# A graph network of four blocks on one core: pooling laid into the attribute pass, and overflow tiles of layer 1 made by comparison

## The chip, the core and the metric

The kernel runs as one program on one core of a Trainium2 chip. The metric is the device time of one execution in microseconds, the median of several runs. The engines are TensorE (PE in the profile), VectorE (DVE), ScalarE (ACT), GpSimd (POOL) and SyncE (SP). SP, and here ScalarE too, issue DMAs whose descriptors the hardware makes; GpSimd issues the indirect DMAs.

## What is computed

There are 12500 nodes with 64 features and 212500 edges, sorted by destination. Every block normalises the node rows, computes, and adds its result to x:

```python
h = relu(layernorm(x)); x = x + L0(h)  # max over edges in both directions of relu(h[.] * (1 + coef*w) @ pool_w.T + b),
                                       # then relu(concat(h, max) @ final_w.T + final_b)
h = relu(layernorm(x)); x = x + L1(h)  # 4 layers: relu(norm(dinv * A^T (dinv * h @ W) + ...)), statistics over all nodes
h = relu(layernorm(x)); x = x + L2(h)  # sums over edges of relu parts of h[dst], vector v and edge weight, then W4
h = relu(layernorm(x)); x = x + L3(h)  # sum, max and mean of 32 edge attributes per source node, then two matrices
```

## The kernel before, in words

Nodes are laid out as NJ = 98 blocks of P = 128 rows, edges as TILES = 1664 columns of 128, worked in NCH = 208 chunks. `adj` in HBM holds the number of edges from source row to destination column as bytes, with NV = 7 further blocks of 128 "virtual" rows. A byte holds up to 255, so for each full 256 equal edges an overflow entry goes to a virtual row; that row stands for one source node (`srow`) and one column (`vcol`, -1 where there is none).

In order of time:

1. Edge pass 1 (GpSimd gathers, L854) and edge pass 2 (GpSimd scatters records, L908), until 4490.
2. GpSimd then works down one queue without a branch: 84 gathers of run ends, `adj_out` for the first 15 of NB = 52 batches (L934; a batch is 32 indirect DMAs of 128 one-byte writes each), a wait for edge pass 3, 98 gathers of run ends into AG, `adj_out` to batch 48, `virtual_rows` (seven gathers of the layer's table at `srow`, after a wait for the table), and the last four batches. When half of a batch is issued it waits for the one before to have landed and counts it in `cells_in`.
3. Beside it the other engines do edge pass 3, then the attribute pass: for each of 208 chunks SP loads records and, for each pair, masks; TensorE turns them (`attr_fwd`), ScalarE makes penalties from the masks (`attr_pen`), VectorE runs two scans of 512 columns (`attr_scans`), TensorE turns back (`attr_back`), ScalarE copies, SP stores. `RUNS_E` cuts the pass after 40 chunks. Between the two parts stands `project`: for 14 groups of seven blocks, `make_b` corrects the run maxima in T and AG and writes Z, TensorE turns Z, ScalarE copies, TensorE multiplies by `finalw`, `post_b` adds to X. Then `norm(NG2 + 2)` on VectorE.
4. Layer 1 in parts (`by_parts` on TensorE, L1322). `CUTS` divides the 98 source blocks into NCK = 9 parts of 30, 16, 14, 12, 8, 6, 5, 5 and 2 blocks (numbered 0 to 8 here). For each part and each of NG2 = 7 groups of 1792 columns (a unit), SP loads one raw tile of 128 x 1792 bytes for each block (L770), ScalarE (three of five, L1808) or VectorE (two of five, L2556/L2558) casts it to bf16 in a ring of NR = 5, and TensorE multiplies it with three bf16 terms, 12 matmuls. SP holds the loads of a part back until `cells_in` reaches a count `chk`, which for this graph is 17, 26, 33, 40, 44, 47, 50, 52 for parts 0 to 7 and NB + 1 = 53 for part 8. `add_part` on VectorE adds a unit's result to FM; for the units of part 8 `scaled` adds, multiplies with the broadcast 1/sqrt(degree) (DINVB, loaded by SP in `group_end`, which waits for `scaled` of the unit two before) and takes statistics. The seven virtual blocks are in part 8: 9 tiles a unit there, 63 in all. Layer 1 has 7 x 105 = 735 tiles.
5. Layers 2 to 4 (`dense`, L1342), then blocks L2 and L3 (L1532). Before the last phase VectorE writes `srj`, the column numbers shifted for each block, with 98 small tensor_scalars (L2796); there the virtual destination tiles are already made by a comparison of `iota_f` with `srj` (L2886).

Before part 8 VectorE's cast is a scalar_tensor_tensor that adds a column of zeros held in PSUM; in part 8 it is a tensor_copy:

```python
if r * NR + i >= LAST_FROM:
    dve.tensor_copy(RING[i], RAW[i]).then_inc(sem("conv_d"), 1)
else:
    dve.scalar_tensor_tensor(RING[i], RAW[i], 1.0, NOTHING.broadcast_to([P, 2 * QW]), ALU.mult, ALU.add)...
```

## Time and profile before

| | us |
|---|---|
| median of three runs | 9879.17 (9872.16 to 9879.8) |
| profiled execution | 9849.77, its span 9847.9 |
| busy in the span: PE, DVE | 7048.5, 7017.6 |
| busy in the span: POOL, ACT | 5374.9, 4868.2 |
| mean granted clock of TensorE | 0.77 |

All durations below are from that one profiled execution, in microseconds from the start of its span. A busy engine doesn't set the time by being busy: one asks in each stretch which engine or transfer the others wait for. "Idle before" is how long an engine sat idle before an instruction, with what released it.

### The profile page before, as it was taken

What the parts mean: (1) busy time and instruction counts of PE and PEld (TensorE: products, weight loads), DVE (VectorE), ACT (ScalarE), POOL (GpSimd) and SP (SyncE); (2) the same over time, 40 slices, a digit from 0 to 9 for tenths busy, and PEclk for the clock granted to TensorE, in tenths of its full rate; (3) what the DMA queues carried; (4) which work ended last, traced back from release to release, by engine and by line L of the source; (5) the groups of instructions that cost most, each with busy time, mean ns of one, the idle gap of its engine ahead of it and who ended that gap; (6) DMA issues with size and microseconds to landing.
All of it is one profiled execution on the core that took longest, in us unless ns stands there. A gap on an engine that the chain in (4) does not pass through costs nothing.

```text
span 9847.9 us, 151767 instructions
## 1 busy us (share of the span) xinstructions
PE 7048.5 (72%) x44134; PEld 5763.7 (59%) x44134; DVE 7017.6 (71%) x18590; ACT 4868.2 (49%) x7967; POOL 5374.9 (55%) x5426
## 2 busy tenths in 40 slices
PE   4444444424888878872656567996899999997998
PEld 3333333313666667661445455664699898896887
DVE  7888888833666666662558777775688787787777
ACT  1111111112555555551442336885688787785787
POOL 5777777777777777777777777776000000000220
PEclk5555555555777776775776788998999999998999
DMA  5556544444333333339995896775788888886999
GB/s 192 195 194 196 175 143 143 144 134 66 93 92 93 92 93 93 94 92 93 266 229 123 188 216 175 204 204 123 221 281 281 248 280 252 275 281 177 210 218 198
DMA packets 2775520, 1739.57 MB, mean 177 GB/s; under 512 B 1805046, under 2 KB 2613980, under 8 KB 2774660
## 3 DMA queue, kind: packets, MB, share of 16 engines
q1 hardware_dynamic: 2435460, 1298.36, 52.3%
q10 hardware_dynamic: 165920, 277.72, 8.1%
q0 software_dynamic: 173408, 154.46, 6.8%
q8 instruction: 370, 6.06, 0.3%
q14 instruction: 362, 2.97, 0.1%
HBM read 1065.70 MB, written 506.69 MB: 160 GB/s over the span
## 4 chain that ended last, share of the span: by engine, by line
POOL 44%; PE 19%; issue 18%; DMA 9%; DVE 5%; ACT 3%; SPq 1%; POOLq 0%; DVEq 0%; ACTq 0%
POOL adj L934 16%; POOL records L908 13%; PE PS L1342 13%; POOL G L854 12%; DMA raw_f<-adj 3%; PE PS L1532 3%; DMA pair_raw<-adj 2%; DVE OH L2136 1%; ACT ring_f L1848 1%; DMA G<-node_table,IDX 1%; POOL fill_rows L870 1%; POOL T L885 1%; ACT ring_f L1971 1%; PE PS L1322 1%; POOL AG L885 1%
## 5 line engine op out<-in xcount | busy, mean ns | idle before, releaser
L854 POOL DMA_INDIRECT G<-node_table,IDX x1664 | 1626.1, 977 | 561.8 <-issue 551.3
L934 POOL DMA_INDIRECT adj<-OH,EA x1664 | 1652.5, 993 | 507.3 <-issue 507.3
L908 POOL DMA_INDIRECT records<-RT,IDX x1664 | 1614.0, 970 | 516.8 <-issue 499.6
L1342 PE MATMUL PS<-ring_f,terms_r 128*128 128x448 f32 x8232 | 1702.6, 368 | 17.3 <-DVE ring_f L2669 8.2
L2669 DVE CAST ring_f<-raw_f 128x1792 fp32r<-128x1792 uint8 x1323 | 1408.0, 1091 | 377.7 <-DMA raw_f<-adj 198.6
L1848 ACT CAST ring_f<-raw_f 128x1792 fp32r<-128x1792 uint8 x882 | 1465.5, 1691 | 380.0 <-DMA raw_f<-adj 249.5
L1342 PEld LDWEIGHTS PS<-ring_f,terms_r 128*128 128x128 f32 x8232 | 1537.3, 188 | 172.0 <-ACT ring_f L1848 19.3
L1187 PE MATMUL PS<-R 98*128 98x128 f32 x3328 | 995.1, 392 | 0.0
L2143 DVE TENSOR_TENSOR_SCAN S<-M,S,PS 128x512 f32<-128x512 bf16 x621 | 791.2, 1274 | 249.0 <-ACT PS L1737 224.2
L1102 PE MATMUL PS<-OH 128*98 128x128 bf16 x3328 | 453.3, 316 | 624.0 <-DVE OH L2136 624.0
L951 POOL DMA_INDIRECT HC<-node_table,srow x21 | 31.2, 1486 | 1510.4 <-issue 1510.4
L1102 PEld LDWEIGHTS PS<-OH 128*98 128x98 bf16 x3328 | 365.7, 198 | 781.8 <-DVE OH L2136 781.8
L2136 DVE TENSOR_SCALAR OH<-iota_b,AG 128x128 bf16<-128x128 bf16 (+1 forms) x4480 | 821.5, 283 | 0.0
L1638 ACT ACTIVATE PS<-PS,poolb 128x512 f32<-128x512 f32 x208 | 137.7, 662 | 1311.1 <-PE PS L992 1068.4
L2558 DVE SCALAR_TENSOR_TENSOR AG<-AG,PS 128x1792 bf16<-128x1792 uint8 x269 | 543.1, 2022 | 275.6 <-PE PS L1322 142.5
L2273 DVE TENSOR_TENSOR L<-PS,below 128x512 bf16<-128x512 f32 x416 | 285.7, 687 | 625.4 <-PE PS L1171 619.0
L968 POOL DMA_INDIRECT ends_b<-runs_e,endrow_src x98 | 144.4, 1474 | 1050.6 <-PE PS L1354 548.7
L1187 PEld LDWEIGHTS PS<-R 98*128 98x128 f32 x3328 | 715.3, 265 | 0.0
L1185 PE MATMUL PS<-OH 128*98 128x128 bf16 x1664 | 474.4, 285 | 316.6 <-ACT R L1672 314.9
L992 PE MATMUL PS<-ident,RT 128*128 128x128 f32 x832 | 232.0, 434 | 597.3 <-DVE RT L2160 592.7
L1532 PE MATMUL PS<-ring_f,terms_r 128*128 128x448 f32 x2744 | 608.9, 376 | 66.6 <-DVE ring_f L2883 31.5
L1971 ACT CAST ring_f<-pair_raw 128x1792 fp32r<-128x1792 uint8 x343 | 571.5, 1692 | 167.0 <-PE PS L1532 111.4
(416 smaller groups left out, 14498.8 us busy)
## 6 DMA issues: line engine op xcount, KB each, us to landing
raw_f<-adj SPq DMA_DIRECT2D x2205, 224.0 KB, 3.7
adj<-Z ACTq DMA_DIRECT2D x105, 1568.0 KB
AG<-adj SPq DMA_DIRECT2D x735, 224.0 KB
G<-records SPq DMA_DIRECT2D x624, 128.0 KB
M<-same_dst SPq DMA_DIRECT2D x416, 128.0 KB
fill_rows<-Z ACTq DMA_DIRECT2D x104, 512.0 KB, 2.8
runs_l<-R SPq DMA_DIRECT2D x208, 256.0 KB
G<-fill_rows SPq DMA_DIRECT2D x208, 256.0 KB
```

What stands on the lines that cost most here:

```text
L854: pool.indirect_dma_start(G[:, i, q * D:(q + 1) * D], None, table, bass.IndirectOffsetOnAxis(ap=IDX[:, i, q:q + 1], axis=0)).then_inc(sem( ...
L908: pool.indirect_dma_start(rec, bass.IndirectOffsetOnAxis(ap=IDX[:, i, q:q + 1], axis=0), RT[:, i, q, :], None).then_inc(sem(f"scattered{i} ...
L934: pool.indirect_dma_start(adj_cells, bass.IndirectOffsetOnAxis(ap=CELL[:, at:at + 1], axis=0), VAL[:, at:at + 1], None).then_inc(sem(f"cel ...
L1102: t = pe.matmul(hist_of(b, k % 2 if b == 0 else 0), OH[:, s, 2 * b, k, 0:NJ], OH[:, s, 2 * b + 1, k, :], start=False, stop=False, skip_gro ...
L1187: t = pe.matmul(bank(6 + x)[:, k * P:(k + 1) * P], OHTs[0:NJ, x, k * P:(k + 1) * P], Cs[0:NJ, k, :], start=False, stop=True, skip_group_ch ...
L1342: m = pe.matmul(half_of(x, h)[:, c, :], stat, RINGF[q % NR][:, h * QW + c * HW:h * QW + (c + 1) * HW], start=K == 0, stop=False, skip_grou ...
L1532: m = pe.matmul(half_of(0, h)[:, c, :], stat, RINGF[n % NE][:, h * QW + c * HW:h * QW + (c + 1) * HW], start=p == 0, stop=p == AB - 1, ski ...
L1848: act.copy(RINGF[q % NR][:, :], RAWF[q % NW][:, :]).then_inc(sem("conv_a"), 1)
L1971: act.copy(RINGF[n % NE][:, :], raw[:, 0:2 * QW, K % 2]).then_inc(sem("conv_a"), 1)
L2136: t = dve.tensor_scalar(OH[:, s, d, k, 0:w], iota_b[:, 0:w], key(d, q + k), None, ALU.is_equal)
L2143: return dve.tensor_tensor_scan(S[:, i % 2, :], mask, data, init, op0, op1)
L2669: dve.tensor_copy(RINGF[q % NR][:, :], RAWF[q % NW][:, :]).then_inc(sem("conv_d"), 1)
```

## The change

The stage `project` between the two parts of the attribute pass goes. The pass runs from 0 to 208 in one piece, and from chunk 40 on each group of nodes is pooled within ten chunks: after chunk 0 of ten the correction of T, after 1 that of AG, after 2 the writing of Z (with TensorE's turn and ScalarE's copy), after 3 the product, after 4 `post_b`. After chunk 180 stand `norm` and its root. PSUM banks 0, 1 and 2 of `project` are replaced by 6, 7 and 4; for that the pass turns back into banks 2 and 3 alone, waiting for the copy of the chunk before, and two of its buffers move from G to S.

In layer 1 the 49 tiles of virtual blocks move from part 8 to part 2 and are no longer loaded: VectorE makes each by comparing, in one scalar_tensor_tensor of 128 x 1792, `iota_f` plus the group's first column with `srj`. Only VectorE's places of the ring take them. The gathers `virtual_rows` move from batch 48 to batch `EV_AT` = 36. `srj` is written for them by four small operations at `srow`, and the 98 tensor_scalars before the last phase become one operation. The closing of units (`add_part`, `scaled`) in parts 7 and 8 stands between casts rather than after a round of five.

```diff
--- before.py
+++ after.py
...
+    EV_C = 2
+    EV_AT = NB * 9 // 13
...
-        RUNS_E = [(0, NCH // 10 * 2), (NCH // 10 * 2, NCH)]
+        POOL_FROM, POOL_STEP = NCH // 10 * 2, 10
+        POOL_END = POOL_FROM + NG * POOL_STEP
+        assert POOL_END < NCH
+        def pooled(d):
+            g, q = divmod(d - POOL_FROM, POOL_STEP)
+            return (g, q) if 0 <= g < NG else (None, None)
...
-        PART = [list(range(CUTS[c], CUTS[c + 1])) + (list(range(NJ, AB)) if c == NCK - 1 else []) for c in range(NCK)]
         UNIT = [(c, g) for c in range(NCK) for g in range(NJ // (2 * GT))]
-        LAST_OF = [sum(len(PART[c]) for c, _ in UNIT[:u + 1]) - 1 for u in range(len(UNIT))]
+        def rows_of_units():
+            units, n = [], 0
+            for c, _ in UNIT:
+                nodes, events, rows = list(range(CUTS[c], CUTS[c + 1])), list(range(NJ, AB)) if c == EV_C else [], []
+                while nodes or events:
+                    rows.append((events if rows and events and n % NR in BY_DVE else nodes).pop(0))
+                    n += 1
+                units.append(rows)
+            return units
+        PART = rows_of_units()
...
-        VIRT_AT = LAST_OF[NJ // (2 * GT) * (NCK - 1) - 1] // NR
+        VIRT_AT = LAST_OF[NJ // (2 * GT) * EV_C - 1] // NR
...
-            attr_run(*RUNS_E[0])
-            sp.wait_ge(sem("zo_used"), QB + NG)
-            attr_run(*RUNS_E[1])
+            attr_run(0, NCH)
...
+                        if K < NJ:
+                            sp.dma_start(RAW[i], adj[K * P:(K + 1) * P, g * (2 * QW):(g + 1) * (2 * QW)]).then_inc(sem(f"ring_in{i}"), 16)
+                        else:
+                            sp.sem_inc(sem(f"ring_in{i}"), 16)
...
-            adj_out(NB // 4 + 2, NB - 4)
+            adj_out(NB // 4 + 2, EV_AT)
             virtual_rows(0, VT)
-            adj_out(NB - 4, NB)
+            adj_out(EV_AT, NB)
...
-                if positive(d - 1):
-                    pe.wait_ge(sem("e_ready"), d - 1)
+                if positive(d):
+                    pe.wait_ge(sem("e_ready"), d)
...
-            attr_run(*RUNS_E[0])
-            pe.wait_ge(sem("e_ready"), RUNS_E[0][1])
-            project(2 * D, finalw[:, :], QB)
-            pe.wait_ge(sem("zo_used"), QB + NG)
-            attr_run(*RUNS_E[1])
+            attr_fwd(0, 0)
+            for d in range(NCH):
+                if d + 1 < NCH:
+                    attr_fwd(d + 1, (d + 1) % 2)
+                attr_back(d, d % 2)
+                g, q = pooled(d)
+                if q == 2:
+                    pool_turned(g)
+                if q == 3:
+                    pool_projected(g)
...
+            then(dve.tensor_scalar(vrow[:, :], row_f[:, :], 0.0, None, ALU.is_ge))
+            then(dve.scalar_tensor_tensor(vcol[:, :], vcol[:, :], 1.0, vrow[:, :], ALU.add, ALU.mult))
+            then(dve.tensor_scalar(vcol[:, :], vcol[:, :], -1.0, None, ALU.add))
+            then(dve.scalar_tensor_tensor(srj.rearrange("p (k j) -> p k j", j=2 * GT), rowbc(iota_f[:, 0:2 * GT], NV), float(-P),
+                                          bc(vcol[:, :], [P, NV, 2 * GT]), ALU.mult, ALU.add))
...
+            def pool_carry(g, t, i, row):
                 j = g * GT
-                ga, gb = group(AG, g), group(T, g)
-                step = then
                 cc = f3(CARG)
-                if positive(g + (QB - 1)):
-                    dve.wait_ge(sem("zo_used"), g + (QB - 1))
-                dve.wait_ge(sem(f"ends{s}"), (g - s) * (8 * GT) + 16 * GT * (NG // 2 + 1))
-                for t, i, row in ((gb, 0, CR[:, :]), (ga, 1, CR2[:, :])):
-                    step(dve.tensor_tensor(cc, rowbc(row, GT), bc(span[i][:, bass.ds(j, GT)], [P, GT, D]), ALU.mult))
-                    step(dve.tensor_tensor(t, t, bc(has[i][:, bass.ds(j, GT)], [P, GT, D]), ALU.mult))
-                    step(dve.tensor_tensor(t, t, cc, ALU.max))
-                z = z3(s, 2 * D)
+                if g:
+                    dve.wait_ge(sem("zo_used"), g)
+                dve.wait_ge(sem(f"ends{g % 2}"), (g - g % 2) * (8 * GT) + 16 * GT * (NG // 2 + 1))
+                then(dve.tensor_tensor(cc, rowbc(row, GT), bc(span[i][:, bass.ds(j, GT)], [P, GT, D]), ALU.mult))
+                then(dve.tensor_tensor(t, t, bc(has[i][:, bass.ds(j, GT)], [P, GT, D]), ALU.mult))
+                then(dve.tensor_tensor(t, t, cc, ALU.max))
+            def pool_joined(g):
+                if g >= 2:
+                    dve.wait_ge(sem("zt"), g - 1)
+                z = z3(g % 2, 2 * D)
                 dve.tensor_scalar(z[:, :, 0:D], group(Hn, g), 1.0, None, ALU.mult)
-                return dve.tensor_tensor(z[:, :, D:2 * D], ga, gb, ALU.max)
-            dve.wait_ge(sem("carry"), 32)
+                dve.tensor_tensor(z[:, :, D:2 * D], group(AG, g), group(T, g), ALU.max).then_inc(sem("z_ready"), 1)
...
-            project(QB, make_b, post_b)
-            norm(NG2 + 2)
-            dve.sem_inc(sem("h_ready"), 1)
-            for d in range(*RUNS_E[1]):
-                attr_scans(d, d % 2, False)
...
+            dve.wait_ge(sem("carry"), 32)
+            for d in range(NCH):
+                attr_scans(d, d % 2, d == 0)
+                g, q = pooled(d)
+                if q == 0:
+                    pool_carry(g, group(T, g), 0, CR[:, :])
+                if q == 1:
+                    pool_carry(g, group(AG, g), 1, CR2[:, :])
+                if q == 2:
+                    pool_joined(g)
+                if q == 4:
+                    dve.wait_ge(sem("zo"), g + 1)
+                    post_b(g).then_inc(sem("zo_used"), 1)
+                if d == POOL_END:
+                    dve.wait_ge(sem("zo_used"), NG)
+                    norm(NG2 + 2)
+                    dve.sem_inc(sem("h_ready"), 1)
...
+                    while ended[0] < len(UNIT) and LAST_OF[ended[0]] + NR <= r * NR + i:
+                        close(ended[0])
+                        ended[0] += 1
+                    if r * NR + i in EVENT:
+                        g, k = EVENT[r * NR + i]
+                        dve.wait_ge(sem("ring_free"), r * NR + (i + 1))
+                        dve.scalar_tensor_tensor(RING[i].rearrange("p (j c) -> p j c", c=P), rowbc(iota_f[:, :], 2 * GT), float(g * 2 * QW),
+                                                 bc(srj[:, k * 2 * GT:(k + 1) * 2 * GT], [P, 2 * GT, P]),
+                                                 ALU.add, ALU.is_equal).then_inc(sem("conv_d"), 1)
+                        continue
...
-            for k in range(NV):
-                for j in range(2 * GT):
-                    t = dve.tensor_scalar(srj[:, k * 2 * GT + j:k * 2 * GT + j + 1], row_f[:, k:k + 1], float(-j * P), None, ALU.add)
-            then(t)
+            then(dve.scalar_tensor_tensor(srj.rearrange("p (k j) -> p k j", j=2 * GT), rowbc(iota_f[:, 0:2 * GT], NV), float(-P),
+                                          bc(row_f[:, :], [P, NV, 2 * GT]), ALU.mult, ALU.add))
```

## Rows read from the trace of the kernel before

**Rows 1.** The page, the chain that ended last: share of the span by engine.

```profile
POOL 44%; PE 19%; issue 18%; DMA 9%; DVE 5%; ACT 3%; SPq 1%; POOLq 0%; DVEq 0%; ACTq 0%
```

**Rows 2.** Groups by line, 6045:6872 and 5302:5402: count | busy us, mean ns | idle before.

```profile
L934 POOL DMA_INDIRECT adj<-OH,EA x643 | 622.9, 969 | 196.0 <-issue 196.0
...
L934 POOL DMA_INDIRECT adj<-OH,EA x57 | 61.9, 1086 | 17.4 <-issue 17.4
```

**Rows 3.** Timeline of VectorE and GpSimd: start, duration, instruction, [idle before <-releaser].

```profile
6758.38 2.02 DVE L2558 SCALAR_TENSOR_TENSOR AG<-AG,PS 128x1792 bf16<-128x1792 uint8 x1 [31.63 <-DMA AG<-adj]
6839.74 2.02 DVE L2558 SCALAR_TENSOR_TENSOR AG<-AG,PS 128x1792 bf16<-128x1792 uint8 x1 [33.05 <-DMA AG<-adj]
...
6871.03 0.97 POOL L934 DMA_INDIRECT adj<-OH,EA  x1 [0.31 <-issue]
```

**Rows 4.** Windows: length, busy us and instructions by engine; PEclk, DMA share, GB/s.

```profile
5302.00:5402.00 100.00, 69.80 (x294) 61.78 (x294) 89.78 (x151) 12.67 (x14) 77.78 (x73) 0.50 0.05 9
...
5440.00:5985.00 545.00, 344.02 (x2057) 279.19 (x2057) 419.06 (x344) 214.58 (x516) 415.40 (x426) 0.84 0.88 207
...
6045.00:6728.00 683.00, 680.35 (x7192) 454.25 (x7190) 522.38 (x279) 590.58 (x358) 519.58 (x537) 1.00 0.72 202
...
6757.00:6812.00 55.00, 49.94 (x714) 32.16 (x714) 35.21 (x21) 34.62 (x21) 41.89 (x44) 0.93 0.50 144
...
6877.00:6910.00 33.00, 4.90 (x24) 1.81 (x24) 5.04 (x3) 4.38 (x3) 0.00 (x0) 0.57 0.81 43
6910.00:6997.00 87.00, 81.20 (x816) 47.86 (x816) 55.23 (x59) 64.86 (x42) 0.00 (x0) 0.97 0.72 219
```

**Rows 5.** Waits, 5440:5985: engine and line <- releaser, us in total, times, longest.

```profile
DVE RT L2476 <- DMA M<-same_src: 101.7, 82, 3.2
```

**Rows 6.** Timeline of TensorE and VectorE in part 8.

```profile
6918.38 0.92 PE L1322 MATMUL PS<-AG,T 128*64 128x512 bf16 x8
...
6933.28 1.08 DVE L2596 TENSOR_TENSOR Hn<-PS,Hn 128x896 f32<-128x896 f32 x1
6934.40 1.09 DVE L2597 TENSOR_TENSOR Hn<-Hn,Z 128x896 f32<-128x896 f32 x1
6935.52 1.15 DVE L2605 BATCH_NORM_STATS2 BN<-Hn 128x6 f32<-128x512 f32 x2
```

**Rows 7.** DMA issues, 6860:6920: KB each, median us from issue to landing.

```profile
Z<-dinv_n SPq DMA_DIRECT2D x1, 224.0 KB, 3.9
```

**Rows 8.** Groups of VectorE by line and form, 8985:9847.

```profile
L2886 DVE TENSOR_TENSOR ring_f<-iota_f,below 128x1792 fp32r<-128x1792 f32 x49 | 99.0, 2021 | 14.2 <-PE PS L1532 13.5
L2796 DVE TENSOR_SCALAR below<-row_f 128x1 f32<-128x1 f32 x98 | 6.0, 146 | 0.0
```

**Rows 9.** Timeline of VectorE in layer 1.

```profile
6584.44 2.02 DVE L2558 SCALAR_TENSOR_TENSOR AG<-AG,PS 128x1792 bf16<-128x1792 uint8 x1 [1.38 <-PE PS L1322]
6586.70 2.02 DVE L2558 SCALAR_TENSOR_TENSOR AG<-AG,PS 128x1792 bf16<-128x1792 uint8 x1 [0.25 <-PE PS L1322]
...
6590.11 2.02 DVE L2558 SCALAR_TENSOR_TENSOR AG<-AG,PS 128x1792 bf16<-128x1792 uint8 x1 [0.38 <-PE PS L1322]
```

**Rows 10.** Timeline of GpSimd and VectorE: indirect DMAs beside long VectorE operations.

```profile
5408.84 6.69 DVE L2073 TENSOR_TENSOR Hn<-X,nd 128x6272 f32<-128x6272 f32 x1
5409.67 6.70 POOL L934 DMA_INDIRECT adj<-OH,EA  x1 [0.30 <-issue]
...
5430.62 6.69 DVE L2079 SCALAR_TENSOR_TENSOR Hn<-Hn,nd 128x6272 f32<-128x6272 f32 x1
5431.04 7.12 POOL L934 DMA_INDIRECT adj<-OH,EA  x1 [0.30 <-issue]
...
6040.35 3.95 DVE L2558 SCALAR_TENSOR_TENSOR AG<-AG,PS 128x1792 bf16<-128x1792 uint8 x2 [0.82 <-DVE PS L2647]
6040.79 0.97 POOL L934 DMA_INDIRECT adj<-OH,EA  x1 [0.30 <-issue]
```

More of the change, by code:

```diff
@@ L763, in _ @@
                 for g in range(NG2):
-                    for K in PART[c]:
+                    for K in PART[c * NG2 + g]:
                         i, r = n % NR, n // NR
@@ L2647, in _ @@
             then(dve.memset(NOTHING, 0.0))
-            AFTER = {(LAST_OF[u] + NR) // NR: u for u in range(len(UNIT) - 1)}
-            assert len(AFTER) == len(UNIT) - 1
+            AFTER = {(LAST_OF[u] + NR) // NR: u for u in range(len(UNIT) - NG2 - 1)}
+            assert len(AFTER) == len(UNIT) - NG2 - 1
+            ended = [len(UNIT) - NG2 - 1]
             for r in range(NG2 * NK):
@@ L2654, in _ @@
                 if r in AFTER:
-                    if UNIT[AFTER[r]][0] < NCK - 1:
-                        add_part(AFTER[r])
-                    else:
-                        scaled(AFTER[r])
+                    add_part(AFTER[r])
+            while ended[0] < len(UNIT) - 1:
+                close(ended[0])
+                ended[0] += 1
             statistics(0, scaled(len(UNIT) - 1))
```

134 lines of the change are left out of this document (45 added, 89 removed).

## The prediction

> **What bounds the kernel now.** I read the chain that ended last first [rows 1]: 44% of it is GpSimd, and the largest line in it is L934, the 1664 indirect DMAs that count edges into `adj`. Their row over 6045 to 6872 [rows 2] shows 969 ns busy and 0.30 us of issue each (622.9 + 196.0 us over 643): 1.27 us apiece, back to back, waiting for nothing. So from 4490, where the second edge pass ends, to the last one at 6871.03 [rows 3] the kernel is as long as GpSimd's queue. The attribute pass, the pooling stage and the start of layer 1 run beside it.
>
> The stages [rows 4] tell who waits. Pooling is 5302 to 5402 with norm after it to 5438, the rest of the attribute pass is 5440 to 5985. Layer 1's first six parts (602 of its 735 tiles) run from 6045 to 6728 with TensorE 680.35 of 683 us busy: 1.134 us a tile. Then TensorE stands: part 6 gets its first tile at 6758, after VectorE sat 31.63 us for a raw tile, and part 7 at 6839.7 after 33.05 us [rows 3]. These are the gates on landed cells (50 and 52 counts), so on GpSimd. Parts 7 and 8 end the stage: 35 + 63 tiles, with a stretch at 6877 to 6910 where TensorE is busy 4.90 of 33 us while raw tiles arrive slowly [rows 4]. What moves time here is only (a) when GpSimd ends and (b) the work that must come after that.
>
> **Pooling moved into the attribute pass.** Removed: a stage of 100 us [rows 4]. Its instructions all stay: 14 groups, each six products and maxima, the two writes of Z, 14 weight products, three steps of `post_b`; VectorE was busy 89.78 us with them. They now stand behind scans. In 545 us of that pass VectorE is busy 419, and 101.7 us of its idle time is waiting for masks [rows 5]. Masks are asked for only when the pair two back is scanned, so work between the scans of a pair delays the request, while work behind the second hides in the wait. If all of the 89.78 us is absorbed, layer 1 starts about 100 us sooner; if none, 10 us. I take 50. SP's queue loses its wait for `zo_used`; TensorE and ScalarE get 14 and 7 small operations between chunks, at 63% TensorE load (344 of 545). A transpose result now waits for the copy of the chunk before, which is under a microsecond of a 3.25 us chunk.
>
> On the path this start is worth **nothing** by itself. Cover: GpSimd's gates. Parts 0 to 5 would now be 602 + 49 = 651 tiles, 738 us; even begun at 6045 they end at 6783, part 6 (35 tiles and the diagonal, 55 us by its stretch) at 6838, and part 7's gate opened at 6839.7 before anything is added to GpSimd. If GpSimd ended much sooner, the start would matter.
>
> **Event tiles moved from part 8 to part 2.** Removed from behind the last gate: 49 of 63 tiles. From the first tile of part 8 at 6918.4 [rows 6] to the end of the stretch at 6997 [rows 4] are 78 us. What stays is 14 tiles and seven closings (`scaled`), each 1.08 + 1.09 + 1.15 us on VectorE [rows 6] with some 0.9 us of casts: 4.3 us a unit against 2.3 us of TensorE, so VectorE and the broadcast of dinv set it. SP loads dinv for unit g+2 only after unit g is scaled, and the raw tiles of g+3 behind that. DMA landing 3.9 us [rows 7], cast, two tiles, closing: some 12.5 us for three units. Seven units come to 30 to 37 us with the head, 33 taken. **Saved: 45 us** (38 to 48).
>
> Added in part 2: 49 comparisons on VectorE, at the price of the same comparison later in the kernel, 2.021 us [rows 8], where the cast was 2.02 [rows 9]. TensorE's pace of 5.67 us per five tiles hides two of them (4.04), and their loads disappear. POOL's seven gathers move from batch 48 to batch 36, near 6210 (16 batches of 32 DMAs, 650 us, before the last). They wait for layer 1's table, which is written before 6045, and land well before part 2, which starts no earlier than 6300 by 322 tiles. So that wait costs nothing.
>
> **What the comparison does to GpSimd.** This is the term that decides. Two long VectorE operations with both inputs in SBUF show it: one started at 5408.84 and took 6.69, so ended at 5415.53; GpSimd's DMA that began at 5409.67 took 6.70 instead of 0.97, ending at 5416.37, 0.84 behind. The scalar_tensor_tensor at 5430.62 did the same (7.12) [rows 10]. The cast of layer 1, whose second input is in PSUM, did not: 0.97 at 6040.79 inside one [rows 10]. So GpSimd loses the VectorE end minus its own start minus 0.13. The new comparison has iota_f and srj, both SBUF, and falls while GpSimd is the bound.
>
> The Trainium skill, "SBUF — State Buffer", section "Who interferes with whom", says that an instruction with two SBUF inputs contends only with a GpSimd instruction that reads SBUF, and infers that descriptor generation is not stalled by tensor_tensor. By that inference the term would be zero and the change would gain the whole tail. These rows disagree with it for indirect DMAs.
>
> Loss per comparison: at chance phase it is 2.02 less 0.15 less half of 1.27, so 1.24 us; at worst 1.87, at best 0.6. But the operations come in step: 2.27 and 3.40 us apart in turn [rows 9]. Followed through: one ends at 2.02, GpSimd's next try is 1.27 later at 3.29, inside the second (2.27 to 4.29), loss 1.00; tries at 5.56 (free) and 6.83, inside the third (5.67 to 7.69), loss 0.86. So 0.93 on the mean, 46 us for 49, and 2 more as each of seven units starts out of step: 48. Pooling's short operations cost GpSimd 57 x (1.086 - 0.969), 7 us [rows 2]; spread, eight a group of 0.62 us each, they cost about 9 by chance phase. **GpSimd ends 50 us later** (bounds 37 at 0.75 each, 79 at 1.5).
>
> **One more edit.** The 98 tensor_scalars of srj before the last phase take 6.0 us [rows 8] while TensorE waits for VectorE's tiles; one operation of 98 elements (0.2 to 0.3 us) takes their place: -5.8 us. The four small operations at srow are beside GpSimd's queue: none.
>
> **Sum**, on the profiled span 9847.9: +50 - 45 - 6 = -1, a span of 9847. Everything after layer 1 only shifts. The profiled execution is 29 us below the median of the runs (9849.77 against 9879.17); I carry the difference over: **9878 us**. Whether the slow loads at 6877 to 6910 belong to the kernel or to that execution doesn't change the sum, as part 7 keeps its place behind its gate in both.
>
> **Rivals.**
> - *GpSimd isn't held by the comparison* (or barely). For it: the page above, and that the operation writes bf16 and reads both inputs with step 0, which no row has together. Against: the two forms in [rows 10]. Then +2 - 45 - 6 = -49, and the start of layer 1 matters a little (part 6 would end at 6838 less 50, before its gate at 6839.7): 9830.
> - *GpSimd is held out of step*, each comparison costing 1.5 us, as one extra try falls into the lock in each turn. The margin is 0.1 to 0.2 us (a try at 5.56 before 5.67). Place: part 2, 6300 to 6550. 49 x 1.5 + 5 = 79, net +28; at 75 it is +24: 9903. It decides from 71 us in all, 1.4 each.
> - *The attribute pass grows*: pooling's steps between the scans of a pair delay its masks request by request. It turns slower only if layer 1 starts over 52 us later than now (part 6 ending past 6890, part 7's new gate), the pass growing by 152 us where 90 us of work is inserted. At 80 later: +28, 9905.
> - *The path was not GpSimd's*: then the 50 us of an earlier start count too: 9878 - 50 - 50 = 9778. Against it: the waits at 6758 and 6839.7.
>
> **How the numbers follow.** Main case 0.60, 9878, own range 9858 to 9902. Not held 0.14, 9830. Out of step 0.17, 9903. Attribute pass 0.05. Not GpSimd's path 0.04. About 0.2% (20 us) is what a measurement of this kernel can tell from no change. Faster: 0.14 + 0.04 + 0.04 of the main case's edge = 0.22. Slower: 0.17 + 0.05 + 0.03 = 0.25. Same 0.53. The range 9850 to 9920 takes in the bounds of the comparison's cost and leaves out the case where nothing is held.
>
> **What would show it.** In the profile after: the stage of 100 us gone and layer 1 starting near 5995; 49 comparisons of 2.02 us in part 2, and L934's kind during them with durations of 1.8 to 2.0 us in place of 0.97, some 48 us in sum; the last of them near 6921; the gaps before parts 6 and 7 longer than 31 and 33 us; from part 8's first tile to the statistics some 33 us; the small tensor_scalars gone. I am wrong if L934's durations stay at 0.97 during the comparisons, if they sum to over 70 us, or if TensorE doesn't wait before part 7.

## The result, and the profile after

| | before | after |
|---|---|---|
| median of 14 runs each, on the same chips | 9879.31 us | 9901.28 us |
| span of the profiled execution | 9847.9 us | 9896.0 us |

The ratio on record is **1.0019, interval 1.0012 to 1.0026**, which is 19 us (12 to 26) slower; the two medians as they stand lie 22 us apart. The forecast was 9878 us and no change. The main line of the forecast held (GpSimd is the bound, and its row of writes is 50 us longer); its tail did not. One execution of a run below took 18677 us at a granted clock of 0.297 and is left out of that run's ratio.

GpSimd's own indirect DMAs of the kernel after come first: the group of all 1664 (xcount, duration min/median/max in ns, first and last start), then the group inside 6300:6600, where the comparisons run, and inside 6570:6900, where they no longer do. They answer to [rows 2] and the last line of [rows 3].

```profile
L958 POOL DMA_INDIRECT adj<-OH,EA x1664: 965/969/7119, 4574.9 to 6916.5; - x185
...
L958 POOL DMA_INDIRECT adj<-OH,EA x197 | 240.3, 1220 | 60.1 <-issue 60.1
...
L958 POOL DMA_INDIRECT adj<-OH,EA x260 | 251.9, 969 | 79.3 <-issue 79.3
```

The row of writes runs from 4574.9 to 6916.5, 2341.6 us. In the kernel before, the same group runs from 4579.3 to 6871.0, 2291.7. So it is 50 us longer, and 197 writes at 1220 instead of 969 ns make up 49 of them. Timelines of GpSimd and of VectorE show one beside the other (start, duration):

```profile
6363.26 1.72 POOL L958 DMA_INDIRECT adj<-OH,EA  x1 [0.30 <-issue]
6365.28 1.96 POOL L958 DMA_INDIRECT adj<-OH,EA  x1 [0.30 <-issue]
6367.55 0.97 POOL L958 DMA_INDIRECT adj<-OH,EA  x1 [0.30 <-issue]
6368.82 1.83 POOL L958 DMA_INDIRECT adj<-OH,EA  x1 [0.31 <-issue]
6370.96 1.97 POOL L958 DMA_INDIRECT adj<-OH,EA  x1 [0.30 <-issue]
...
6364.38 2.03 DVE L2545 SCALAR_TENSOR_TENSOR AG<-iota_f,below 128x1792 bf16<-128x1792 f32 x1 [0.24 <-PE PS L1335]
...
6367.79 2.02 DVE L2545 SCALAR_TENSOR_TENSOR AG<-iota_f,below 128x1792 bf16<-128x1792 f32 x1 [0.38 <-PE PS L1335]
6370.06 2.02 DVE L2545 SCALAR_TENSOR_TENSOR AG<-iota_f,below 128x1792 bf16<-128x1792 f32 x1 [0.24 <-PE PS L1335]
```

The rhythm is the one that was worked out: free, held by 0.86, held by 1.00.

VectorE's first casts of parts 6 and 7 answer to the first lines of [rows 3], and the two `add_part` rows of part 6 below show its units:

```profile
6802.87 2.02 DVE L2554 SCALAR_TENSOR_TENSOR AG<-AG,PS 128x1792 bf16<-128x1792 uint8 x1 [71.06 <-DMA AG<-adj]
...
6821.93 1.08 DVE L2639 TENSOR_TENSOR Hn<-PS,Hn 128x896 f32<-128x896 f32 x1
...
6829.89 1.08 DVE L2639 TENSOR_TENSOR Hn<-PS,Hn 128x896 f32<-128x896 f32 x1
...
6884.92 3.95 DVE L2554 SCALAR_TENSOR_TENSOR AG<-AG,PS 128x1792 bf16<-128x1792 uint8 x2 [30.07 <-DMA AG<-adj]
```

The wait before part 6 has grown from 31.63 to 71.06 us: there the sooner start and the 50 us of GpSimd lie. The units of part 6 are 7.96 us apart (6821.93 to 6829.89), where they were 6.85 us apart before (closings at 6768.97 and 6775.82 in the kernel before). Nothing in the forecast had that.

Windows of the kernel after answer to [rows 4]: the attribute pass between its first pooling and its end, layer 1 up to part 5, the gap before part 6, the stretch behind GpSimd's last write, and part 8. The columns are those of [rows 4].

```profile
5440.00:5910.00 470.00, 274.83 (x1746) 231.41 (x1746) 408.52 (x375) 165.54 (x395) 363.29 (x351) 0.83 0.80 183
5995.00:6738.00 743.00, 737.02 (x7778) 455.46 (x7772) 561.70 (x301) 638.76 (x390) 577.04 (x545) 1.00 0.68 185
6757.00:6802.00 45.00, 0.00 (x0) 0.00 (x0) 0.00 (x0) 0.00 (x0) 34.03 (x37) 0.50 0.03 3
6917.00:6955.00 38.00, 8.71 (x78) 4.23 (x72) 4.65 (x4) 5.05 (x3) 0.45 (x1) 0.66 0.82 39
6968.60:7016.60 48.00, 26.15 (x216) 13.39 (x212) 32.01 (x38) 13.38 (x8) 0.00 (x0) 0.83 0.52 148
```

Two things are to be seen in the last two rows. After the last write TensorE again does nearly nothing for 38 us (8.71 busy) while the DMA engines are 82% busy and move 39 GB/s. And part 8, priced at 33 us, takes 48.0. (The forecast counted from the part's first tile on TensorE, 6918.4 in the kernel before; the 48.0 here and all figures of part 8 below count from its first cast on VectorE, 6914.9 there. By this count the price is some 36.5.) The waits of VectorE in 5340:5914 answer to [rows 5], which has 5440:5985: masks now cost 56.9 us, 101.7 before.

```profile
DVE RT L2456 <- DMA M<-same_src: 56.9, 47, 2.9
```

The account from GpSimd's last write to the aggregate of the statistics is then 6871.0 to 6997.3 before, 126 us, and 6916.5 to 7016.6 after, 100 us. The change saved **26 us** there in this pair of executions, not 45. (Two runs below with the same tail, column numbers in PSUM and events alone, had 96.1 and 93.0 us there, which makes it 30 and 33.) With +50, and GpSimd's first write 4.4 us sooner in this execution (it starts anywhere from 4575 to 4592 in the runs below), layer 1 ends 19.3 us later, 7016.6 for 6997.3, which is the size of the result. The spans of the two executions lie 48 us apart, since the execution before was also short behind layer 1: 2850.7 us from the aggregate to the end of the span, 2879.4 after.

### The profile page after: what moved, and what is told of

It reads as the page before. It is cut to its first block, busy times and chain, and to the rows that moved or that the text cites. A ratio compares the mean times of both kernels' runs of the same rounds, so it can differ in the third digit from the quotient of the medians.

```text
span 9896.0 us, 151652 instructions
## 1 busy us (share of the span) xinstructions
PE 7048.5 (71%) x44134; PEld 5722.6 (58%) x44134; DVE 7024.0 (71%) x18497; ACT 4876.6 (49%) x7967; POOL 5424.5 (55%) x5426
## 4 chain that ended last, share of the span: by engine, by line
POOL 42%; issue 18%; PE 14%; DMA 13%; DVE 7%; ACT 4%; SPq 2%; POOLq 0%; ACTq 0%; DVEq 0%
POOL adj L958 17%; POOL records L932 12%; POOL G L878 11%; PE PS L1355 8%; DMA raw_f<-adj 5%; DMA pair_raw<-adj 3%; PE PS L1545 2%; ACT ring_f L1850 2%; DVE OH L2111 2%; DMA G<-node_table,IDX 1%; DMA IDX<-in_src_q 1%; ACT ring_f L1973 1%; DMA records<-RT,IDX 1%; POOL fill_rows L894 1%; POOL AG L909 1%
## 5 line engine op out<-in xcount | busy, mean ns | idle before, releaser
L958 POOL DMA_INDIRECT adj<-OH,EA x1664 | 1703.9, 1024 | 507.3 <-issue 507.0
L2554 DVE SCALAR_TENSOR_TENSOR AG<-AG,PS 128x1792 bf16<-128x1792 uint8 x239 | 482.1, 2021 | 309.5 <-DMA AG<-adj 174.2
```

The costliest lines, as they stand in the source:

```text
L958: pool.indirect_dma_start(adj_cells, bass.IndirectOffsetOnAxis(ap=CELL[:, at:at + 1], axis=0), VAL[:, at:at + 1], None).then_inc(sem(f"cel ...
```

## The experiments

My theory after the two traces: the comparisons hold GpSimd by 50 us; of the 45 us of the tail, 8 were lost to longer units in parts 6 and 7 and 11 to a last part that is longer than priced; and both kernels lose some 30 us behind GpSimd's last write to something that isn't in the change. The rivals: the comparison isn't the cause of the 50; the pooling has a share in the result; what is won ahead of layer 2 is given back.

Each ratio is to the kernel before, measured on the same chip in the same job. "Write row" is from GpSimd's first to its last write, "to statistics" from that last write to the aggregate, "part 8" from its first cast on VectorE to the aggregate, all in us of the profiled execution.

| run | ratio (interval) | write row | to statistics | part 8 |
|---|---|---|---|---|
| before | 1 | 2291.7 | 126.3 | 82.4 |
| after | 1.0019 (1.0012 to 1.0026) | 2341.6 | 100.1 | 48.0 |
| column numbers in PSUM | 0.9969 (0.9957 to 0.9980) | 2292.6 | 96.1 | 47.1 |
| closings between casts | 1.0019 (1.0010 to 1.0028) | 2338.1 | 93.4 | 48.9 |
| three writes of padding less | 0.9998 (0.9989 to 1.0007) | 2337.5 | 86.0 | 47.6 |
| the same in the kernel before | 0.9982 (0.9973 to 0.9991) | 2288.4 | 116.4 | 83.0 |
| pooling alone | 1.0001 (0.9992 to 1.0010) | 2289.8 | 129.8 | 81.6 |
| events alone | 1.0012 (1.0003 to 1.0021) | 2344.4 | 93.0 | 47.3 |
| padding spread | 0.9999 (0.9990 to 1.0008) | 2348.3 | 77.8 | 46.8 |
| SyncE's order | 1.0007 (0.9998 to 1.0016) | 2341.3 | 84.1 | 34.7 |
| all padding dropped | 0.9983 (0.9974 to 0.9992) | | | |
| four edits | 0.9915 (0.9901 to 0.9928) | 2289.0 | 48.7 | 33.1 |
| four without closings | 0.9926 (0.9913 to 0.9940) | 2290.2 | 56.9 | 33.8 |
| before, two edits | 0.9971 (0.9961 to 0.9981) | 2286.6 | 106.4 | 88.9 |

### Is it the comparison that holds GpSimd?

```diff
             then(dve.memset(NOTHING, 0.0))
+            IOTA_P = PS[:, 5 * 512:5 * 512 + P]
+            then(dve.tensor_copy(IOTA_P, iota_f[:, :]))
...
-  dve.scalar_tensor_tensor(RING[i]..., rowbc(iota_f[:, :], 2 * GT), float(g * 2 * QW),
+  dve.scalar_tensor_tensor(RING[i]..., rowbc(IOTA_P, 2 * GT), float(g * 2 * QW),
```

> The changed kernel with one edit: the 49 comparisons of layer 1 read the row of column numbers from a copy in PSUM instead of from SBUF, so that only one of their inputs lies in SBUF. Theory (GpSimd is held by the comparisons and is the bound up to its last write of the adjacency): those writes go back to a mean of 993 ns over all 1664 (969 ns while the comparisons run, not 1220), GpSimd ends 45 to 48 us sooner than in the changed kernel (6916.5, so about 6870), and the whole time falls by the same, from 9901 to about 9856, 23 us under the kernel before. Rival 1 (the writes are held by something else, such as the pooling that is spread over the attribute pass): their mean stays near 1024 ns and the time stays at 9901. Rival 2 (the writes do go faster, but what comes after the last gate, or the statistics, does not start sooner): GpSimd ends near 6870 and the time stays above 9890.

Measured: 9859.5 us beside 9889.3 of the kernel before, ratio 0.9969; against the 1.0019 of the change that is 0.0050 or 49 us. The groups of GpSimd in 6300:6600, and the two engines beside each other:

```profile
L958 POOL DMA_INDIRECT adj<-OH,EA x236 | 229.3, 972 | 72.0 <-issue 72.0
...
6371.32 0.97 POOL L958 DMA_INDIRECT adj<-OH,EA  x1 [0.31 <-issue]
6372.59 0.97 POOL L958 DMA_INDIRECT adj<-OH,EA  x1 [0.30 <-issue]
6373.87 0.97 POOL L958 DMA_INDIRECT adj<-OH,EA  x1 [0.30 <-issue]
...
6372.46 2.02 DVE L2545 SCALAR_TENSOR_TENSOR AG<-PS,below 128x1792 bf16<-128x1792 f32 x1 [0.25 <-PE PS L1335]
```

The comparison takes the same 2.02 us, and the writes inside it are back at 0.97. One operand moved to PSUM is worth 49 us in the row of writes (2341.6 to 2292.6, 2291.7 in the kernel before) and 49 us in the time, within an interval of some 13 us. This settles the first question: nothing else of the change lengthens GpSimd's row, and the time follows it. The Trainium skill, "SBUF — State Buffer", section "Who interferes with whom", infers that descriptor generation is not stalled by `tensor_tensor`; by this pair of runs GpSimd's indirect DMAs are stalled by a scalar_tensor_tensor with both tensors in SBUF, and the measurement decides. The rule beside that inference, that two SBUF inputs contend with a GpSimd instruction that reads SBUF, agrees with the pair if an indirect DMA counts as one, its offsets lying in SBUF; no run here tests that.

### Which half of the change?

The kernel before with the pooling hunks of the diff alone, and with the event hunks alone.

> The kernel before with the pooling laid into the attribute pass as in the changed kernel, and nothing else: the overflow tiles of layer 1 are still loaded, in the last part. Theory (the bound up to the last gate is GpSimd's row of writes, which does not look at the attribute pass): layer 1 starts about 50 us sooner (5988 instead of 6040), the waits before the gates grow by as much, GpSimd's last write comes at 6871 give or take 5, and the time is that of the kernel before, ratio 0.999 to 1.001. Rival 1 (the pooling's operations, spread thinly, hold GpSimd or lengthen the pass more than the stage did): ratio 1.001 to 1.003, which would be a part of the 22 us of the change. Rival 2 (the sooner start does help, since the early parts run ahead): ratio below 0.999.

> The kernel before with its pooling stage as it was, and only the overflow tiles changed: made by comparison in the units of part 2 and taken from the last part. Theory (the whole result comes from this half): the writes are held for 45 to 50 us by the 49 comparisons, GpSimd ends 45 to 50 us later than in the kernel before, the stretch from its last write to the statistics falls from 125 to about 99 us, and the ratio is that of the whole change, 1.001 to 1.003 (9890 to 9908). Rival (the two halves work on each other, since the units of part 2 fall on another stretch of GpSimd's row when layer 1 starts 50 us later): the comparisons hold fewer writes, and the ratio lies under 1.001, or over 1.003.

Pooling alone: 1.0001, layer 1's first cast at 5986.5 instead of 6040.4, GpSimd's last write at 6867.6. Fifty microseconds sooner in layer 1 are worth nothing, as the gates had it, and spreading the pooling costs GpSimd nothing that can be seen: its row is 2 us shorter than before, where 2 more had been expected. Events alone: 1.0012, row of writes 52.7 us longer. Within the intervals the two add up to the whole change, and no effect of one half on the other is seen.

### Why is the tail worth 26 us and not 45? The units of parts 6 and 7

```diff
-  AFTER = {(LAST_OF[u] + NR) // NR: u for u in range(len(UNIT) - NG2 - 1)}
-  ended = [len(UNIT) - NG2 - 1]
+  AFTER = {(LAST_OF[u] + NR) // NR: u for u in range(len(UNIT) - 3 * NG2)}
+  ended = [len(UNIT) - 3 * NG2]
```

> The changed kernel with one edit: the units of parts 6 and 7 are closed between two casts, as soon as the cast that would need their last tile's buffer comes up, as those of part 8 are, instead of after a whole turn of the ring. Theory (the move of 49 tiles out of the last part shifted where a unit's last tile falls in the ring of five buffers, so that TensorE now waits 1.1 us in each unit of parts 6 and 7 for the sum of the unit two back): the units of part 6 take 6.8 us and those of part 7 5.7 us again instead of 7.96 and 6.79, and since part 7 stands behind the last gates by most of its length the time falls by 5 to 8 us, to 9893 to 9896. Rival (the longer units come from the transfers, which share the queues with GpSimd's last writes): the units keep 7.96 and 6.79 us and the time stays at 9901.

TensorE's timeline of the kernel after shows what the edit is about: at the head of each unit it stands for `add_part` (L2639). Below it, VectorE's timeline of the run with the edit:

```profile
6815.12 0.95 PE L1335 MATMUL PS<-AG,T 128*64 128x512 bf16 x8 [0.91 <-DVE Hn L2639]
...
6823.07 0.95 PE L1335 MATMUL PS<-AG,T 128*64 128x512 bf16 x8 [0.92 <-DVE Hn L2639]
```

```profile
6828.38 1.09 DVE L2639 TENSOR_TENSOR Hn<-PS,Hn 128x896 f32<-128x896 f32 x1 [0.18 <-PE PS L1335]
6829.59 2.02 DVE L2554 SCALAR_TENSOR_TENSOR AG<-AG,PS 128x1792 bf16<-128x1792 uint8 x1
6833.03 2.02 DVE L2554 SCALAR_TENSOR_TENSOR AG<-AG,PS 128x1792 bf16<-128x1792 uint8 x1 [1.42 <-PE PS L1335]
6835.23 1.09 DVE L2639 TENSOR_TENSOR Hn<-PS,Hn 128x896 f32<-128x896 f32 x1 [0.18 <-PE PS L1335]
```

The units are 6.85 us apart again and `add_part` comes 0.18 us after TensorE's last product. So the mechanism stands: the table `AFTER` puts a unit's sum behind the last cast of a turn of the five buffers; with 49 tiles moved ahead, each of these units ends in another buffer of the turn, and one cast more stands before the sum. The time did not follow: 1.0019, as without it. The stretch from the last write to the statistics is 93.4 us where the change had 100.1, but the run of the events alone has 93.0 there with the old closings: one profile doesn't tell. From the last cast of the layers to the last cast of the last phase this run takes 896.9 us and the kernel after 892.0, and the nine profiled executions that have the same code there differ by 18.6 us. Beside the three other edits, where the padding no longer stands in the way (see below), the same closings give 48.7 against 56.9 us from the last write to the statistics, and 0.9915 against 0.9926 in the time, 11 us; the two intervals overlap. So some 8 us are shown in the trace of that pair; in the time they are not resolved.

### The last part

```diff
                 else:
+                    group_end(0, 0, 0)
+                    group_end(1, 1, 1)
                     sp.wait_ge(sem("cells_in"), NB + 1)
                 for g in range(NG2):
...
-                    if c == NCK - 1:
-                        group_end(g, g, g % 2)
+                    if c == NCK - 1 and g >= 3:
+                        group_end(g - 1, g - 1, (g - 1) % 2)
+            group_end(NG2 - 1, NG2 - 1, (NG2 - 1) % 2)
```

> The changed kernel with one edit, in the order of SyncE's list in the last part: the factors of its first two units are loaded before the last gate, and the tiles of each unit are put before the wait for an earlier unit's closing instead of behind it. Theory (the step of the prediction that was mis-sized: it priced the last part at 33 us, but SyncE holds each unit's two tiles back until the unit two before it is closed, which costs a transfer of 4 us in every unit): the last part, from its first cast to the statistics, falls from 48.0 us to 33 to 35, as in the run that had this edit among four, and the time falls by about 14 us to a ratio of 1.0005 give or take 0.0008. Rival (the part was short in that run because the padding's writes no longer stood in the way, not because of SyncE's order): it stays at 46 to 48 us, and the ratio at 1.002.

SyncE's queue and VectorE's timeline in part 8 of the kernel after:

```profile
6978.92 1.06 SPq L792 DMA_DIRECT2D AG<-adj  x2
6986.93 1.09 SPq L763 DMA_DIRECT2D Z<-dinv_n  x2
6988.07 1.05 SPq L792 DMA_DIRECT2D AG<-adj  x2
...
6975.54 1.09 DVE L2592 TENSOR_TENSOR Hn<-PS,Hn 128x896 f32<-128x896 f32 x1
...
6983.68 1.09 DVE L2552 CAST AG<-AG 128x1792 bf16<-128x1792 uint8 x1 [4.74 <-DMA AG<-adj]
6984.69 1.08 DVE L2592 TENSOR_TENSOR Hn<-PS,Hn 128x896 f32<-128x896 f32 x1
...
6988.01 1.07 DVE L2592 TENSOR_TENSOR Hn<-PS,Hn 128x896 f32<-128x896 f32 x1
...
6996.33 1.09 DVE L2552 CAST AG<-AG 128x1792 bf16<-128x1792 uint8 x1 [4.94 <-DMA AG<-adj]
6997.34 1.08 DVE L2592 TENSOR_TENSOR Hn<-PS,Hn 128x896 f32<-128x896 f32 x1
```

A ring is to be read in them: unit 0 is closed (6975.54), then SyncE issues the tiles of unit 3 (6978.92), these are cast 4.74 us late (6983.68), and only behind that cast, in VectorE's own order, unit 1 is closed (6984.69). From the closing of unit 0 to that of unit 3 it takes 21.8 us, where 12.5 had been priced. With SyncE's order changed:

```profile
6977.62 1.09 DVE L2595 TENSOR_TENSOR Hn<-PS,Hn 128x896 f32<-128x896 f32 x1
...
6981.93 1.08 DVE L2595 TENSOR_TENSOR Hn<-PS,Hn 128x896 f32<-128x896 f32 x1
...
6985.67 1.09 DVE L2595 TENSOR_TENSOR Hn<-PS,Hn 128x896 f32<-128x896 f32 x1 [0.34 <-DMA Z<-dinv_n]
...
6990.42 1.08 DVE L2595 TENSOR_TENSOR Hn<-PS,Hn 128x896 f32<-128x896 f32 x1
```

12.8 us for the same three units and 34.7 us for part 8, 13 us less than in the kernel after. The ratio is 1.0007, 12 us less than that of the change, though the two intervals overlap. The forecast's price was that of a kernel whose SyncE doesn't hold the tiles back.

### What stalls both kernels behind the last write

The kernel after and the kernel before without their last three writes (384 of the 492 padding edges, which are written to neighbouring bytes of one row that nobody reads); the changed kernel with these three sent 32 bytes apart, in another of the 128 rows that are kept for what nobody reads; and with all padding edges dropped, which is the first edit below and the last one together.

```diff
-  pool.wait_ge(sem(f"cells{k % 4}"), (k // 4 + 1) * 16 * CB)
+  pool.wait_ge(sem(f"cells{k % 4}"), (k // 4 + 1) * 16 * CB - (48 if k == NB - 1 else 0))
-  for n in range(k * CB, (k + 1) * CB):
+  for n in range(k * CB, min((k + 1) * CB, TILES - 3)):
```

> The changed kernel without the last three of the 1664 writes of the adjacency, which hold only padding edges whose 384 one-byte values all go to the row kept for them; nothing that is computed is left out. Theory (these one-byte writes go to neighbouring bytes of a few lines of memory and are served one after the other, and the loads that are queued on the same DMA rings behind them wait): the load of the last part that now takes 29.7 us to arrive after its gate takes 3 to 5 us, part 8 starts about 30 us sooner, and the time falls by 25 to 35 us, to about 9870. Rival 1 (the stall is the loads' own, or comes from GpSimd's queue being drained of real edges): the wait of about 30 us stays, only the 3.8 us of the three writes go, and the time is 9897. Rival 2 (the padding edges of the fourth last write are enough): the stall is shorter by three quarters only, and the time falls by 20 or less.

> The kernel before without the last three of its 1664 writes of the adjacency (padding edges only; nothing that is computed is left out). In this kernel the loads of the last part waited 28.2 us as well, and its 56 overflow tiles came from the last part's loads. Theory (one-byte writes to the same lines): the wait goes, and the time falls by 25 to 35 us, from 9879 to about 9850. Rival (the stall is not theirs): the time falls by 3.8 us or less. If this kernel gains as much as the changed one does, the stall is no part of the difference between the two; if it gains less, the stall hid part of the tail that the change took away.

```diff
+  pool.iota(AWAY[:, :], [[32, 3]], base=NOWHERE * NP, channel_multiplier=96)
...
-  bass.IndirectOffsetOnAxis(ap=CELL[:, at:at + 1], axis=0), VAL[:, at:at + 1], None)
+  bass.IndirectOffsetOnAxis(ap=CELL[:, at:at + 1] if n < TILES - 3
+                            else AWAY[:, n - TILES + 3:n - TILES + 4], axis=0), VAL[:, at:at + 1], None)
```

> The changed kernel, with its last three writes of the adjacency (384 padding edges) sent to places 32 bytes apart in the row kept for padding, instead of to neighbouring bytes; their number and size are the same, and nothing that is computed is left out. Theory (what stalls the loads of part 8 is that these one-byte writes fall on the same few lines): the load that took 36 us after the gate takes 19 us, as it did without these writes, and the time falls by about 17 us against the changed kernel (ratio to the kernel before about 1.000). Rival (it is the number of the one-byte writes that are still queued, wherever they go): the load takes 36 us as before and the ratio stays near 1.002. Second rival (a wait of some 20 us stays because the fourth last write still holds 108 padding edges): the wait that is left is 15 to 20 us in this run as well.

```diff
   VAL[:, at:at + 1], None
+  , **(dict(bounds_check=NOWHERE * NP - 1, oob_is_err=False) if n >= TILES - 4 else {})
```

> The changed kernel with one edit: the last three writes of the adjacency are left out and the padding edges of the fourth last are dropped (108 of its 128). Nothing that is computed is left out. Theory (the wait of 36 us on the first load behind the last writes is the padding's, 19 us of it were left by the 108 edges of the fourth last write): the wait is 5 us or less, the stretch from GpSimd's last write to the statistics falls from 100 us to about 72, and the time falls by 29 to 35 us, to a ratio of 0.999. Rival (the fourth write brings nothing; the rest of the gain of the combined run came from SyncE's order): a wait of 15 us or more and a ratio of 1.000.

The longest load behind the last write, as the chains of waits have it: after, SyncE's order, three writes less, padding spread, four edits (with all padding dropped). In the first four it brings one of the last tiles of part 7; in the fifth those tiles are not late any more, and the load shown is the first of part 8.

```profile
6918.42 36.32 DMA AG<-adj
```

```profile
6921.07 34.49 DMA AG<-adj
```

```profile
6921.19 19.08 DMA AG<-adj
```

```profile
6941.10 16.46 DMA AG<-adj
```

```profile
6879.64 4.92 DMA AG<-adj
```

The times follow: 1.0019, then 0.9998 with three writes less, 0.9999 with them spread, 0.9983 with all padding dropped (35 us; no profile of it is read). The changed kernel gains 21 us and the kernel before 17 us (0.9982) from three writes less, of which 3.8 us are the three writes' own; the 25 to 35 us expected of both were too much, with 108 padding edges left. The run with the writes spread tells the cause apart: as many one-byte writes, of the same size, in the same queue, and the wait is less than half; so it is not their number but that they fall on neighbouring bytes. When the 108 padding edges of the fourth last write go too, the time falls by 15 us more (0.9998 to 0.9983), and in the profiles of the three runs that drop them (four edits, four without closings, before with two edits) VectorE never waits 4 us for a tile behind the last write. The DMA queues, of which SyncE issues on q1, in 6918:6953 of the kernel after and 6870:6885 of the one with four edits (packets, MB, share of 16 engines):

```profile
DMA packets 919, 1.35 MB, mean 38 GB/s; under 512 B 177, under 2 KB 918, under 8 KB 918
...
q1 hardware_dynamic: 834, 1.33, 81.0%
...
q0 software_dynamic: 84, 0.00, 0.2%
```

```profile
DMA packets 2068, 3.62 MB, mean 241 GB/s; under 512 B 314, under 2 KB 1811, under 8 KB 2067
...
q1 hardware_dynamic: 2003, 3.60, 82.3%
```

The engines are as busy in both, at 38 and at 241 GB/s. An estimate from these rows: a packet of the loads takes 0.54 us of an engine in the first and 0.10 us in the second. The writes of GpSimd are listed under another queue (q0), with 0.2% of the engines' time, so the loads don't wait behind them in one queue, as the first expectation of this section had it. It is the loads' own packets that are slow; what they wait for, and what the memory does with such writes, was not measured. Both kernels have the stall and gain alike from three writes less (21 and 17 us), so no part of the difference between them is seen in it.

### All together, and the kernel before with what fits it

> The changed kernel with four edits: the row of column numbers read from PSUM (48 us by its own run); units of parts 6 and 7 closed between casts (8 us sooner in its trace); the padding edges of the last four writes dropped (21 us by the run without three of them, and up to 15 more for the fourth, which still held 108 such edges); and, in the last part, the factors of the first two units loaded ahead and each unit's tiles loaded before the wait for the unit three back. Nothing that is computed is left out. Theory (all of these lie one behind the other on the chain from GpSimd's row to the statistics, so they add up): 48 + 21 + 8 to 15 + 5, that is 80 to 90 us under the changed kernel, 9815 to 9825 (ratio 0.992 to 0.994). Rival 1 (what is gained ahead of layer 2 is given back in layers 2 to 4, as for the closings, whose run was no faster): ratio 0.995 to 0.997. Rival 2 (the stall after the last write is not the padding's alone, so the fourth write brings nothing more): ratio 0.993 to 0.995 with a wait of 15 us or more left on the first load behind the gate.

> The combined kernel without its edit of the closings of parts 6 and 7: comparisons with the column numbers in PSUM, the padding edges dropped, and SyncE's order changed in the last part. Theory (the ring's phase costs 1.1 us in each unit of the last stretch behind the gate): it is 7 to 8 us slower than the combined run, ratio 0.9923 against 0.9915, and its units of parts 6 and 7 take 7.96 and 6.79 us against 6.8 and 5.7. Rival (the closings are worth nothing in the time, as their own run had it, since a sooner start of layer 2 is given back): ratio 0.9915, with units that are longer all the same.

> The kernel before with two of the edits that helped the changed one: the padding edges of the last four writes dropped, and SyncE's order changed in the last part (the comparisons and the closings have no place in it). Nothing that is computed is left out. Its last part takes 82 us and holds all 56 overflow tiles. Theory (what the change moves off the end is worth 34 to 45 us, once its comparisons do not hold GpSimd and the padding does not hide it): the padding's drop brings about 30 us to this kernel as well, and SyncE's order at most 5, since its units of 9 and 16 tiles hide the wait; ratio 0.996 to 0.997, so that the combined kernel stays 40 to 55 us faster than it. Rival (the change gains nothing even with its flaws mended, and all that the combined kernel wins is won by edits that fit the kernel before too): ratio 0.992.

Four edits: 9785.6 us beside 9866.8, ratio **0.9915**, 81 us under the kernel before and some 103 under the changed one. The single runs add up to 49 + 35 + 12 = 96, and the closings' 8 of the trace make it 104; each of these differences is known to some 10 us, so that they meet so closely is partly luck. What is won ahead of layer 2 is not given back. The 80 to 90 us that I expected were too few: SyncE's order was worth 12 and not 5, and the sum had one of its terms fewer than the text names (48 + 21 + 15 + 8 + 5 is 97). From the last write to the statistics it takes 48.7 us, where it was 126. That is faster than both kernels.

The kernel before with the padding dropped and SyncE's order changed: 0.9971. Of the 84 us of the combined kernel, 29 fit the kernel before as well, and 55 need the change. My expectation for it named 40 to 55. Its part 8 takes 88.9 us, where the three profiles with SyncE's old order have 81.6 to 83.0: no gain from the order shows where a unit has 9 tiles. With the new order the factors stand in the queue behind nine tiles, and VectorE waits 13.5 us for them in that part (the load of Z from `dinv_n`), where the old order has no such wait; for tiles it waits 7.7 us and not 22.7.

## Why the prediction was wrong, point by point

- **GpSimd is the bound up to the last gate.** Right. Pooling alone starts layer 1 54 us sooner and moves the time by 0.0001; the PSUM run shortens GpSimd's row and the time by the same 49 us. VectorE still waits before parts 6 and 7 (71.06 and 30.07 us).
- **Pooling absorbed by half, worth nothing.** Right: 52 us sooner for 50 forecast, the wait for masks down from 101.7 to 56.9 us. The 2 us that it was to cost GpSimd didn't show.
- **The comparisons hold GpSimd by 48, +50 in all** (37 to 79). Right: +49.9 in the row of writes, with the 0.86 and 1.00 us of the worked rhythm in the trace. The rival "not held" is out by the PSUM run, the rival "out of step" by the 1220 ns.
- **Part 8 in 33 us.** This is the step that failed: the term of -45. The part measured 48.0 (46.8 to 48.9 in the runs that left it alone) against 82.4 (81.6 to 83.0); saved were 34 us and not 45. The term knew that SyncE loads the tiles of unit g+3 behind the closing of g, but let three units run in that ring. VectorE's order lets only one: the closing of g+1 stands behind the cast of a tile of g+3. Three units cost 21.8 us and not 12.5. With SyncE's order changed they cost 12.8, and the part takes 34.7.
- **Parts 6 and 7 as before.** A second term that was put at zero. The units of parts 6 and 7 take 7.96 and 6.8 us where they took 6.85 and 5.7, in every run with the moved tiles and the old closings. What that costs is less sure while the stall lasts: from the last write to the first cast of part 8 it took 43.9 us before and 48.3 with the pooling alone, against 52.1 after, 49.4 with SyncE's order, 49.0 with the column numbers in PSUM and 45.6 with the events alone, and 44.5 with the closings between casts. With all padding dropped it is 23.0 against 15.5. So it costs 0 to 8 us in the change.
- **The srj operations, -5.8.** A third term that failed: the price was right, the path wasn't. Timelines of VectorE at the head of the last phase, before and after:

```profile
9061.98 6.02 DVE L2796 TENSOR_SCALAR below<-row_f 128x1 f32<-128x1 f32 x98
9068.03 2.10 DVE L2883 CAST ring_f<-pair_raw 128x1792 fp32r<-128x1792 uint8 x2
```

```profile
9093.03 0.26 DVE L2797 SCALAR_TENSOR_TENSOR below<-iota_f,row_f 128x98 f32<-128x98 f32 x1
9093.32 2.09 DVE L2884 CAST ring_f<-pair_raw 128x1792 fp32r<-128x1792 uint8 x2
...
9107.75 1.09 DVE L2884 CAST ring_f<-pair_raw 128x1792 fp32r<-128x1792 uint8 x1 [3.30 <-DMA pair_raw<-adj]
```

From the last cast of the layers to the first of this phase it takes 109.3 to 111.5 us in the four profiles with the old code (mean 110.6) and 103.0 to 105.9 in nine with the new (mean 104.8): the 5.8 us are there. Ten casts later the means are 131.5 and 130.2, and VectorE has waited longer for the loads of the phase's first tiles in between (11.9 us after, 5.8 before). So the loads set the time there, which the forecast left out. To the last cast of the phase it is 872.9 to 888.3 us with the old code (mean 880.5) and 878.3 to 896.9 with the new (mean 885.2), and no gain is left to be seen.
- **Sum.** The forecast's -1 becomes +16 with the two terms as they were measured (+50 for GpSimd, -34 for part 8, nothing for srj), and 16 to 24 with parts 6 and 7; the ratio of 0.0019 means 19 (12 to 26). The time lies inside the range that was given, because the largest term was right; what failed is that gain and loss were said to cancel. The difference of 29 us between the profiled execution of before and its median was rightly carried: from the last cast of the layers to the last of the last phase it took 872.9 us, the shortest of thirteen.
- **The slow stretch at 6877 to 6910.** I called it without effect on the sum, and that holds as far as the runs tell: both kernels have it. But I passed over its cause, and it was the second-largest gain that was to be had, 35 us in the changed kernel.

## What to carry to other kernels

When work is taken out from behind a gate, price what is left by following every engine's own order around the ring once, for one unit: the tiles that hid a wait leave with the work, and here 11 of 45 us went into a wait that nine-tile units had covered. Ask of a saving at the head of a phase whether the loads for it are there: the 5.8 us were gone ten casts later. A comparison that replaces a load is not free for GpSimd while it issues indirect DMAs: give one operand a place in PSUM. And send padding that must be written somewhere to places far apart, or drop it.

## What the runs showed of the hardware that was not expected

- One-byte writes to neighbouring bytes make loads that are issued right behind them slow: 384 of them in three indirect DMAs cost 17 to 21 us (3.8 of them their own), 492 cost 35, at 38 GB/s against 241 without them. The same 384 at 32 bytes apart cost nothing that can be told from leaving them out (0.9999 and 0.9998).
- An operation of VectorE with two inputs in SBUF, both read with repeated elements and with bf16 out, holds GpSimd's indirect DMA until it ends (0.97 to 1.97 us); with the repeated row in PSUM it doesn't, at the same 2.02 us.
- From the last cast of the layers to the last cast of the last phase, nine profiled executions with the same code there took from 878.3 to 896.9 us. A gain of 8 us in the layer before is not to be proved by one profile's span.
